# Attention stage of a fused attention and expert kernel: all 32 pairs written out in place of a loop on the engines

## The chip, the cores and the metric

The kernel runs on one core of a Trainium2 chip. Its engines each run their own instruction stream and meet at semaphores: TensorE (PE), VectorE (DVE), ScalarE (ACT), GpSimd (POOL) and SyncE (SP), the last for transfers alone. The metric is the device time of one execution in microseconds, the median of several runs; lower is better.

## The reference

One layer: cross attention with 16 heads of 8 dimensions over 64 batches of 64 tokens (D = 128), added to the input, and then a mixture of 8 experts with one expert per token, added again.

```python
x = x + xattn(_layernorm(x), ctx, ctx, mask, ...)     # H = 16, DK = 8
x = x + ffn(_layernorm(x), ...)

# xattn
scores = jnp.einsum('bhqd,bhkd->bhqk', q, k) * scale
scores = jnp.where(mask == 0, jnp.float32(-1000000000.0), scores)
attn = jax.nn.softmax(scores, axis=-1)
out = jnp.einsum('bhqk,bhkd->bhqd', attn, v)
return out.transpose(0, 2, 1, 3).reshape(query.shape[0], -1, D) @ Wo.T + bo

# ffn
router_probs = jax.nn.softmax(xt @ Wr + br, axis=-1)
gates = jnp.max(router_probs, axis=-1, keepdims=True)
idx = jnp.argmax(router_probs, axis=-1)
h = jax.nn.relu(jnp.einsum('te,td,edf->tf', onehot, xn, W1) + b1[idx])
y = (jnp.einsum('te,tf,efd->td', onehot, h, W2) + b2[idx]) * gates
```

## The kernel before

The 4096 tokens are worked on in 32 tiles of 128 tokens, each a pair of batches (NP = 32). The attention stage is a software pipeline over steps j: in step j every engine has a body `step(h, u)` with h = j // 2 and u = j % 2, and it works in it on several pairs at once, each in a different state. `pair(h, u, k)` gives the pair j + k, with its turn and its buffer (all tiles of the stage have two buffers).

In one step VectorE does, in this order: the layer norm's statistics of pair j + 3 (L489), the normalized tile xn of pair j + 2 (L495), the second layer norm of pair j - 4 (xt L501, row L503), the routing of pair j - 5 (L511 to L525), the row maxima of the scores of pair j (mx L535) and their subtraction (Pr L539), the division of the attention output of pair j - 2 (L546, L548), the residual and its statistics for pair j - 3 (L561 to L589) and the place in the table of pair j - 5 (L576 to L599). TensorE does the scores of pair j (L677, L681), eight transposes of the probabilities of pair j - 1 (L692), three transposes of xn, On and xt (L706 to L714), the output projection (L723), the router (L726), the ranks (L730, L731), probabilities times values of pair j - 2 (L738) and the projections for q, k and v (L752 to L757). ScalarE copies transposed tiles out of PSUM (L402, L409), takes the exponential (L419) and copies q, k and v (L424 to L434). GpSimd takes powers for the layer norms (rs L325, L336), adds the bias (L330), makes the blocks of k (Kb L341) and issues the indirect DMA that enters a token in a table (L349). SyncE loads x and the context (L226, L230, L234) and stores rows (L241).

The order of each engine is that of the code; nothing is scheduled by a planner. Each producer counts up a semaphore, and a consumer waits for a count that follows from the pair's number, for example `dve.wait_ge(s_s, p + 1)`.

`steps(eng, step, first, main, last, n)` (L49) lays these steps out. Steps before n * main[0] and from n * main[1] on are written out: h and u are numbers, and so are the counts waited for and the addresses. Between them stands a loop on the engine, `eng.Fori(main[0], main[1])`, whose body is n steps; there h is a register, and each count or address that follows from it is computed by the engine's sequencer. For the attention stage AM = (4, 13) and n = 2: nine turns of two steps, j = 8 to 25. Steps j = -3 to 7 and 26 to 36 are written out.

Behind it stands the stage of the experts with its own loops, over 39 slots of 128 tokens (`bstep`, `entries`, from about 296 us on).

Of the kernel before, what the change touches and what calls it, by code (L numbers as in the profile page):

```python
# [27 lines left out]
NP = T // P  # L28
# [14 lines left out]
def wait(eng, sem, value):  # L43

    if not (isinstance(value, int) and value <= 0):
        eng.wait_ge(sem, value)


def steps(eng, step, first, main, last, n):  # L49

    for j in range(first, n * main[0]):
        step(j // n, j % n)
    with eng.Fori(main[0], main[1]) as h:
        for u in range(n):
            step(h, u)
    for j in range(n * main[1], last):
        step(j // n, j % n)


def build(nc, x, ctxT, mask, wqT, bq, wkT, bk, wvT, bv, woT, bo, wr, br, ln_g, ln_b, w1, b1, w2, b2, out):  # L60
# [3 lines left out]
    with ExitStack() as ctx:  # L64
# [141 lines left out]

        block = ctx.enter_context(nc.Block())

        AM, A1 = (4, 13), NP + 5
        B0, BM, B1 = -2, (2, 9), SLOTS + 2  # L210

        def pair(h, u, k):
            p = at(h, u, k, 2)
            return None if isinstance(h, int) and not 0 <= p[0] < NP else p

        def slotn(h, u, k):
            s = at(h, u, k, R)
            return None if isinstance(h, int) and not 0 <= s[0] < SLOTS else s

        @block.sync  # L220
        def _(sp):
            def load(h, u):
                if (t := pair(h, u, 5)):
                    p, n, q = t
                    wait(sp, x_in[q], 16 * n)
                    sp.dma_start(X[:, bass.ds(p, 1), :], x[bass.ds(p * P, P), :].rearrange("t (o d) -> t o d", o=1)).then_inc(x_in[q], 16)  # L226
                if (t := pair(h, u, 4)):
                    p, n, q = t
                    wait(sp, s_pj, p - 1)
                    sp.dma_start(C[:, q, :], ctxT[:, bass.ds(p * P, P)]).then_inc(c_in[q], 16)  # L230
                if (t := pair(h, u, 2)):
                    p, n, q = t
                    wait(sp, s_pj, p + 1)
                    sp.dma_start(Cv[:, q, :], ctxT[:, bass.ds(p * P, P)]).then_inc(cv_in[q], 16)  # L234

            def step(h, u):
                load(h, u)
                if (t := pair(h, u, -4)):
                    p, n, q = t
                    sp.wait_ge(s_xt2, 2 * p + 2)  # L240
                    sp.dma_start(rows[bass.ds(p * P, P), :], row[:, q, :]).then_inc(r_out[q], 16)  # L241

            load(-3, 1)
            sp.dma_start(Wq[:], wqT).then_inc(s_w[0], 16)
            load(-2, 0)
            sp.dma_start(Wk[:], wkT).then_inc(s_w[0], 16)
            sp.dma_start(Wv[:], wvT).then_inc(s_w[0], 16)
            sp.dma_start(Wo[:], woT).then_inc(s_w[0], 16)
            load(-2, 1)
            for e in range(0, E, 2):  # L250
                sp.dma_start(W1[:, e:e + 2, :], w1[e:e + 2].rearrange("e d f -> d e f")).then_inc(s_w[3], 16)
                sp.dma_start(W2[:, e:e + 2, :, :], w2[e:e + 2].rearrange("e (c f) d -> f e c d", c=FC)).then_inc(s_w[3], 16)
            load(-1, 0)
            load(-1, 1)
            steps(sp, step, 0, AM, A1, 2)

            sp.wait_ge(s_slot, 1)
            for q in range(2):
                sp.wait_ge(r_out[q], 16 * (NP // 2))
                sp.wait_ge(e_out[q], 16 * (NP // 2))  # L260

            def entries(h, u):
                if (t := slotn(h, u, 0)):
                    s, n, q = t
                    wait(sp, e_in[q], 16 * n)
                    first = sp.value_load(slot[0:1, 1, bass.ds(s, 1)], min_val=0, max_val=ROWS - P)
                    sp.dma_start(ENT[:, bass.ds(s, 1), :], table[bass.ds(first, P), :].rearrange("t (o d) -> t o d", o=1)).then_inc(e_in[q], 16)

            steps(sp, entries, 0, (1, 9), SLOTS, R)
            for q in range(R):  # L270
                sp.wait_ge(o_out[q], 16 * len(range(q, SLOTS, R)))

        @block.gpsimd
        def _(pool):
# [75 lines left out]
                                         in_=ent[:, q, :], in_offset=None, bounds_check=last_entry,  # L350
                                         oob_is_err=False).then_inc(e_out[q], 16)

            steps(pool, step, -3, AM, A1, 2)

            def bstep(h, u):
                if (t := slotn(h, u, 2)):
# [18 lines left out]
        def _(act):  # L375
# [58 lines left out]
                            a.activation(VB[64 * h2:64 * h2 + 64, q, b, :, h2, 0:DK], src[:, :, h2, :],  # L434
                                         ACT.Copy).then_inc(s_v, 1)

            steps(act, step, -2, AM, A1, 2)

            act.wait_ge(s_slot, 1)
            act.wait_ge(s_w[3], 16 * (E + 2))  # L440
# [20 lines left out]
        def _(dve):  # L461
# [136 lines left out]
                    dve.wait_ge(s_pos, 6 * p + 3)  # L598
                    v.tensor_copy(posi[:, q, :], posf[:, q, :]).then_inc(s_pos, 1)  # L599

            steps(dve, step, -3, AM, A1, 2)


            k = [0]
# [56 lines left out]
        def _(pe):  # L661
# [96 lines left out]
                if last is not None:  # L758
                    last.then_inc(s_pj, 1)

            steps(pe, step, -2, AM, A1, 2)


            pe.wait_ge(s_rt, 7 * NP)
# [68 lines left out]
```

## Time and profile before

| | before |
|---|---|
| median of 3 runs | 470.75 us |
| lowest, highest | 468.31 us, 471.48 us |
| span of the profiled execution | 445.3 us |
| PE, DVE, ACT, POOL busy, share of the span | 75%, 68%, 46%, 47% |
| instructions profiled | 12096 |
| granted TensorE clock, mean | 0.822 |

The span goes from the first to the last instruction of the profiled execution; the time of a run is taken from outside and is longer. The granted clock is given as a share of full speed, 1.00 at 2.4 GHz and 0.50 at 1.2 GHz. Busy shares are means over two stages that have different limits, so a change in the attention stage is read from that stage alone, which takes from about 14 us to 296 us. VectorE's L535 occurs once for each pair, 32 times.

### The profile page before, as it was taken

What the parts mean: (1) busy time and instruction counts of PE and PEld (TensorE: products, weight loads), DVE (VectorE), ACT (ScalarE), POOL (GpSimd) and SP (SyncE); (2) the same over time, 40 slices, a digit from 0 to 9 for tenths busy, and PEclk for the clock granted to TensorE, in tenths of its full rate; (3) what the DMA queues carried; (4) which work ended last, traced back from release to release, by engine and by line L of the source; (5) the groups of instructions that cost most, each with busy time, mean ns of one, the idle gap of its engine ahead of it and who ended that gap; (6) DMA issues with size and microseconds to landing.
All of it is one profiled execution on the core that took longest, in us unless ns stands there. A gap on an engine that the chain in (4) does not pass through costs nothing.

```text
span 445.3 us, 12096 instructions
## 1 busy us (share of the span) xinstructions
PE 335.5 (75%) x2988; PEld 243.7 (55%) x2989; DVE 302.3 (68%) x1120; ACT 202.6 (46%) x588; POOL 207.4 (47%) x261
## 2 busy tenths in 40 slices
PE   0578879879889889898967886406888888888870
PEld 0356647658668668676745665303555655555550
DVE  3268999888988988988999895651454545444440
ACT  1158564644554554545565553001545454544540
POOL 5314354354354354354364523313576666666540
PEclk9999996685785775758699785555999999999996
DMA  5921121111111121111121100002222221122110
GB/s 141 381 70 51 33 52 40 35 55 30 30 59 30 30 59 30 30 53 36 35 45 35 32 25 24 26 0 48 55 53 69 59 60 51 59 65 59 50 31 0
DMA packets 35770, 23.64 MB, mean 53 GB/s; under 512 B 11599, under 2 KB 32724, under 8 KB 35744
## 3 DMA queue, kind: packets, MB, share of 16 engines
q1 hardware_dynamic: 29872, 14.99, 12.0%
q0 software_dynamic: 4272, 7.69, 5.9%
q10 hardware_dynamic: 1600, 0.65, 0.6%
q8 instruction: 12, 0.20, 0.3%
q14 instruction: 14, 0.11, 0.1%
HBM read 16.55 MB, written 7.22 MB: 53 GB/s over the span
## 4 chain that ended last, share of the span: by engine, by line
DVE 30%; issue 29%; PE 17%; POOL 7%; DMA 6%; ACT 3%; DVEq 3%; ACTq 1%; POOLq 1%; SPq 0%
PE ps L776 7%; DVE mx L535 6%; PE ps L784 6%; DMA G<-rows_dram,gi 4%; ACT xg L447 3%; DVE lsub L514 2%; DVE xt L501 2%; POOL rs L336 2%; DVE st L569 2%; DVE row L503 1%; DVE Pr L539 1%; PE ps L792 1%; DVE oh L522 1%; DVE rsum L546 1%; DVE st L489 1%
## 5 line engine op out<-in xcount | busy, mean ns | idle before, releaser
L336 POOL TENSOR_TENSOR rs<-ve,half 128x2 f32<-128x2 f32 x32 | 23.1, 723 | 107.3 <-DVE ve L589 103.9
L419 ACT ACTIVATE Pr<-Pr,rowany 128x1024 f32<-128x1024 f32 x32 | 36.7, 1148 | 65.1 <-DVE Pr L539 65.1
L644 DVE COPY hs<-ps 128x512 f32<-128x512 f32 x39 | 27.0, 692 | 52.3 <-PE ps L776 52.3
L368 POOL DMA_INDIRECT out<-ot,si x39 | 39.5, 1013 | 44.1 <-DVE gi L639 20.5
L776 PE MATMUL ps<-W,xg 128*128 x78 | 45.5, 666 | 17.1 <-ACT xg L447 17.1
L692 PE MATMUL ps<-ident,Pr 128*128 128x128 f32 x256 | 54.1, 350 | 2.0 <-ACT Pr L419 1.7
L784 PEld LDWEIGHTS ps<-W,hT 128*128 128x128 f32 x312 | 38.6, 192 | 25.4 <-issue 25.3
L455 ACT ACTIVATE hT<-ps,b1c 128x128 f32<-128x128 f32 x156 | 44.6, 369 | 16.2 <-PE ps L798 10.3
L402 ACT ACTIVATE PT<-ps 128x512 f32<-128x512 f32 x64 | 38.2, 598 | 26.2 <-PE ps L692 25.7
L692 PEld LDWEIGHTS ps<-ident,Pr 128*128 128x128 f32 x256 | 39.0, 180 | 19.5 <-issue 14.9
L361 POOL DMA_INDIRECT G<-rows_dram,gi x39 | 39.9, 1023 | 18.7 <-issue 11.0
L447 ACT ACTIVATE xg<-ps,cols 128x128 f32<-128x128 f32 x39 | 17.9, 458 | 63.6 <-PE ps L792 63.6
L738 PE MATMUL ps<-VB,PT 128*64 128x18 f32 x1024 | 45.3, 236 | 0.7 <-ACT GT L409 0.7
L784 PE MATMUL ps<-W,hT 128*128 x312 | 43.2, 282 | 0.8 <-ACT hT L455 0.7
L738 PEld LDWEIGHTS ps<-VB,PT 128*64 128x64 f32 x1024 | 42.0, 171 | 1.7 <-ACT GT L409 0.9
L535 DVE TENSOR_REDUCE mx<-ps 128x16 f32<-128x1024 f32 x32 | 39.1, 1221 | 3.0 <-PE ps L681 3.0
L539 DVE TENSOR_TENSOR Pr<-ps,mx 128x1024 f32<-128x1024 f32 x32 | 39.2, 1224 | 2.0
L349 POOL DMA_INDIRECT table_dram<-ent,posi x32 | 34.8, 1088 | 9.1 <-issue 3.7
L341 POOL TENSOR_TENSOR Kb<-KT,hmask 128x512 f32<-128x512 f32 x32 | 33.4, 1044 | 11.8 <-ACT KT L426 11.8
L409 ACT ACTIVATE GT<-ps 128x384 f32<-128x384 f32 (+2 forms) x38 | 16.7, 440 | 41.5 <-PE ps L714 32.0
L325 POOL TENSOR_TENSOR rs<-ve,half 128x1 f32<-128x1 f32 x32 | 18.0, 563 | 36.0 <-DVE ve L530 36.0
L706 PE MATMUL ps<-ident,xn 128*128 128x128 f32 x32 | 11.6, 363 | 24.5 <-DVE xn L495 24.5
(119 smaller groups left out, 679.0 us busy)
## 6 DMA issues: line engine op xcount, KB each, us to landing
W<-in_w SPq DMA_DIRECT2D x8, 512.0 KB, 8.7
rows_dram<-row SPq DMA_DIRECT2D x32, 128.0 KB
X<-in_x SPq DMA_DIRECT2D x32, 64.0 KB, 1.9
C<-in_ctxT SPq DMA_DIRECT2D x32, 64.0 KB
Cv<-in_ctxT SPq DMA_DIRECT2D x32, 64.0 KB, 2.0
ENT<-table_dram SPq DMA_DIRECT2D x39, 1.0 KB
G<-rows_dram,gi POOLq DMA_INDIRECT x39, 2.8
out<-ot,si POOLq DMA_INDIRECT x39, 2.3
```

The lines of the kernel that those rows point to most:

```text
L349: g.indirect_dma_start(out=table, out_offset=bass.IndirectOffsetOnAxis(ap=posi[:, q, :], axis=0), in_=ent[:, q, :], in_offset=None, bounds ...
L361: g.indirect_dma_start(out=G[:, q, :], out_offset=None, in_=rows, in_offset=bass.IndirectOffsetOnAxis(ap=gi[:, q, :], axis=0), bounds_chec ...
L368: g.indirect_dma_start(out=out, out_offset=bass.IndirectOffsetOnAxis(ap=si[:, q, :], axis=0), in_=ot[:, q, :], in_offset=None, bounds_chec ...
L402: a.activation(PT[:, q, 512 * m:512 * m + 512], ps[:, 4 + m, :], ACT.Copy).then_inc(s_pt, 1)
L419: a.activation(Pr[:, q, :], Pr[:, q, :], ACT.Exp, scale=rowany[:, 0:1]).then_inc(s_p, 1)
L455: a.activation(hT[:, q % 2, P * c:P * c + P], ps[:, 2 + q % 2, P * c:P * c + P], ACT.Relu, bias=b1c[:, bass.ds(ex * FC + c, 1)]).then_inc( ...
L535: v.tensor_reduce(out=mx[:, q, :].rearrange("p (g i) -> p g i", i=4), in_=sc, axis=AX.X, op=ALU.max).then_inc(s_sm, 1)
L539: v.tensor_tensor(out=Pr[:, q, :].rearrange("p (g i k) -> p g i k", g=4, k=S), in0=sc, in1=mx[:, q, :].rearrange("p (g i) -> p g i", i=4)[ ...
L692: last = nc.tensor.transpose(ps[:, 4 + m, 128 * j:128 * j + 128], Pr[:, q, 128 * (4 * m + j):128 * (4 * m + j) + 128], ident[:])
L738: last = mm(psPV[64 * b:64 * b + 64, 18 * j:18 * j + 18], PT[:, q, 128 * j + 64 * b:128 * j + 64 * b + 64], VB[:, q, b, j, :, :].rearrange ...
L776: mm(ps[:, q % 2, :], xg[:, q, :], W1[:, bass.ds(ex, 1), :].rearrange("p e f -> p (e f)"), start=True, stop=True).then_inc(b_up, 1)
L784: last = mm(ps[:, 6 + q % 2, 0:D], hT[:, q % 2, P * c:P * c + P], W2[:, bass.ds(ex, 1), c, :].rearrange("p e d -> p (e d)"), start=(c == 0 ...
```

## The change

The loop of the attention stage is taken away on all five engines. Each engine now has all its steps written out with h and u as numbers. The bodies are the same, and the loops of the expert stage stay. The same two lines replace the call of `steps` on SP, POOL, ACT, DVE and PE; the first step is 0, -3, -2, -3 and -2.

```diff
-        AM, A1 = (4, 13), NP + 5
+        A1 = NP + 5
...
-            steps(sp, step, 0, AM, A1, 2)
+            for j in range(0, A1):
+                step(j // 2, j % 2)
...
-            steps(dve, step, -3, AM, A1, 2)
+            for j in range(-3, A1):
+                step(j // 2, j % 2)
```

What this moves is seen in each engine's instructions. First VectorE, at the entry of the loop (step j = 8), kernel before. The rows read line, instruction, output and inputs, and in brackets the semaphores that are waited for; ISA and REGISTER_ALU rows are register work of the sequencer.

```order
L599 CAST posi<-posf 128x1 [waits places]
L53 UNCONDITIONAL_BRANCH
L53 ISA
L489 ISA [waits x_in1]
L489 BN_STATS st<-X 128x6
L490 ISA
L46 REGISTER_ALU [waits ln1_rstd,ln1_stats]
L495 ISA [waits step_transposed]
L495 TENSOR_SCALAR xn<-X,mv,rs 128x128
L499 ISA
L46 REGISTER_ALU [waits ln2_rstd]
L501 TENSOR_SCALAR xt<-row,mv,rs 128x128 [waits step_transposed]
```

The same place in the changed kernel, whose line numbers are three higher here:

```order
L602 CAST posi<-posf 128x1 [waits places]
L492 BN_STATS st<-X 128x6 [waits x_in1]
L498 TENSOR_SCALAR xn<-X,mv,rs 128x128 [waits step_transposed,ln1_rstd,ln1_stats]
L504 TENSOR_SCALAR xt<-row,mv,rs 128x128 [waits step_transposed,ln2_rstd]
L506 TENSOR_SCALAR row<-row,mv,rs 128x128
```

The arithmetic instructions and the semaphores they wait for are the same ones; the branch and the register rows between them are gone.

TensorE at its entry of the loop, kernel before:

```order
L757 MATMUL ps<-Wv,Cv 128x128 [waits cv_in1]
L53 UNCONDITIONAL_BRANCH
L53 ISA
L46 REGISTER_ALU [waits k_blocks,q_copied]
L677 MATMUL ps<-pen,eye 128x256 [waits softmax_shift]
L677 MATMUL ps<-pen,eye 128x256 x3
L681 MATMUL ps<-Kb,QT 64x256 x8
L689 ISA
L46 ISA [waits probs]
L692 MATMUL ps<-ident,Pr 128x128 [waits pT_copied]
L692 MATMUL ps<-ident,Pr 128x128 x3
```

And in the changed kernel, line numbers four higher:

```order
L761 MATMUL ps<-Wv,Cv 128x128 [waits cv_in1]
L681 MATMUL ps<-pen,eye 128x256 [waits softmax_shift,k_blocks,q_copied]
L681 MATMUL ps<-pen,eye 128x256 x3
L685 MATMUL ps<-Kb,QT 64x256 x8
L696 MATMUL ps<-ident,Pr 128x128 [waits pT_copied,probs]
L696 MATMUL ps<-ident,Pr 128x128 x3
```

Here too the matrix products follow in the same order with the same waits; the waits that stood on register rows (k_blocks with q_copied, and probs) now stand on the instructions themselves.

## Rows read from the trace of the kernel before

**Rows 1.** The page, its first line.

```profile
span 445.3 us, 12096 instructions
```

**Rows 2.** Timeline of VectorE, starts of L535: start us, duration us, engine, line.

```profile
67.39 1.21 DVE L535 TENSOR_REDUCE mx<-ps 128x16 f32<-128x1024 f32 x1
...
226.67 1.21 DVE L535 TENSOR_REDUCE mx<-ps 128x16 f32<-128x1024 f32 x1
...
234.08 1.22 DVE L535 TENSOR_REDUCE mx<-ps 128x16 f32<-128x1024 f32 x1
```

**Rows 3.** Stretches: length, busy PE, PEld, DVE, ACT, POOL, clock, DMA, GB/s.

```profile
59.98:67.39 7.41, 5.55 (x78) 4.02 (x76) 7.02 (x31) 4.27 (x14) 3.83 (x5) 1.00 0.19 42
151.60:159.95 8.35, 8.35 (x74) 6.63 (x74) 7.17 (x29) 3.73 (x10) 3.82 (x5) 0.50 0.14 39
159.95:168.43 8.48, 6.43 (x81) 4.97 (x80) 7.56 (x29) 4.88 (x15) 3.82 (x5) 0.90 0.14 39
226.67:234.08 7.41, 5.54 (x78) 4.02 (x76) 7.02 (x30) 4.25 (x14) 3.82 (x5) 1.00 0.19 33
241.49:249.24 7.75, 5.67 (x78) 4.06 (x76) 7.18 (x28) 4.39 (x14) 4.28 (x6) 1.00 0.10 27
249.24:257.01 7.77, 7.70 (x71) 5.88 (x72) 6.91 (x25) 3.53 (x10) 3.31 (x4) 0.56 0.16 44
```

**Rows 4.** Timeline of VectorE, in the loop and behind it; idle before in brackets.

```profile
164.60 0.15 DVE L599 CAST posi<-posf 128x1 int32<-128x1 f32 x1
164.85 0.29 DVE L489 BATCH_NORM_STATS2 st<-X 128x6 f32 x1
165.34 0.93 DVE L495 TENSOR_SCALAR xn<-X,mv,rs 128x128 f32 x1 [0.20 <-DVE st L489]
...
173.56 0.29 DVE L489 BATCH_NORM_STATS2 st<-X 128x6 f32 x1 [0.54 <-issue]
...
230.81 0.14 DVE L599 CAST posi<-posf 128x1 int32<-128x1 f32 x1
230.87 0.28 DVE L489 BATCH_NORM_STATS2 st<-X 128x6 f32<-128x128 f32 x1
...
236.47 0.24 DVE L546 RECIPROCAL rsum<-ps 128x16 f32<-128x16 f32 x1
...
246.34 1.05 DVE L501 TENSOR_SCALAR xt<-row,mv,rs 128x128 f32<-128x128 f32 x1 [0.29 <-POOL rs L336]
```

**Rows 5.** Timeline of TensorE, in the loop at low clock and behind it.

```profile
185.16 1.90 PE L738 MATMUL ps<-VB,PT 128*64 128x18 f32 x32
...
193.98 1.90 PE L738 MATMUL ps<-VB,PT 128*64 128x18 f32 x32
...
229.28 0.59 PE L677 MATMUL ps<-pen,eye 64*128 64x256 bf16 x4 [0.60 <-DVE Pr L539]
...
231.68 0.30 PE L706 MATMUL ps<-ident,xn 128*128 128x128 f32 x1 [0.59 <-DVE xn L495]
...
232.62 0.33 PE L714 MATMUL ps<-ident,xt 128*128 128x128 f32 x1 [0.54 <-DVE xt L501]
...
234.12 1.11 PE L738 MATMUL ps<-VB,PT 128*64 128x18 f32 x32
```

**Rows 6.** Stretches before, in and behind the loop, columns as in group 3.

```profile
24.30:68.50 44.20, 36.95 (x472) 26.91 (x472) 38.06 (x115) 28.53 (x77) 19.03 (x27) 1.00 0.16 44
...
75.40:218.70 143.30, 126.12 (x1276) 99.08 (x1276) 125.16 (x477) 73.56 (x204) 64.92 (x85) 0.69 0.14 39
218.70:249.50 30.80, 22.98 (x313) 16.77 (x313) 28.96 (x112) 17.82 (x51) 15.82 (x21) 1.00 0.15 36
```

**Rows 7.** DMA queues: packets, MB, share; 24:68, then 84:218, then landings.

```profile
q8 instruction: 4, 0.07, 0.5%
q14 instruction: 3, 0.02, 0.2%
...
q14 instruction: 1, 0.01, 0.0%
...
X<-in_x SPq DMA_DIRECT2D x32, 64.0 KB, 1.9
```

More of the change, by code:

```diff
@@ L351, in step @@
                                          oob_is_err=False).then_inc(e_out[q], 16)
-            steps(pool, step, -3, AM, A1, 2)
+            for j in range(-3, A1):
+                step(j // 2, j % 2)
             def bstep(h, u):
@@ L435, in step @@
                                          ACT.Copy).then_inc(s_v, 1)
-            steps(act, step, -2, AM, A1, 2)
+            for j in range(-2, A1):
+                step(j // 2, j % 2)
             act.wait_ge(s_slot, 1)
@@ L599, in step @@
                     v.tensor_copy(posi[:, q, :], posf[:, q, :]).then_inc(s_pos, 1)
-            steps(dve, step, -3, AM, A1, 2)
+            for j in range(-3, A1):
+                step(j // 2, j % 2)
             k = [0]
@@ L759, in step @@
                     last.then_inc(s_pj, 1)
-            steps(pe, step, -2, AM, A1, 2)
+            for j in range(-2, A1):
+                step(j // 2, j % 2)
             pe.wait_ge(s_rt, 7 * NP)
```

## The prediction

> **What bounds the kernel now.** I read the page first for where the time lies. The profiled execution spans 445.3 us [rows 1]; the median of the runs is 470.75 us (468.31 to 471.48), so 25.45 us lie outside the span, and I take them as untouched. Then I took the vector engine's timeline and followed one instruction, the maximum over the scores (L535). It runs once per step, so its starts are the clock of the attention stage. Where the same steps are written out, behind the loop, one takes 234.08 - 226.67 = 7.41 us [rows 2]. Next to it I put the table by stretches, with the starts of L535 as bounds, so that each row is one step [rows 3]. The reader is to see two paces in it: 7.41 us with VectorE busy for 7.02 of them where steps are written out, and 8.35 and 8.48 us with 7.17 and 7.56 busy for the two steps of a turn of the loop (16.83 us, 8.41 a step). Written-out steps leave VectorE 0.4 us of idle time, the loop's 1.0 us on average.
>
> Third, what fills that time. In a written-out step the statistics of the next tile (L489) start 0.06 us after the cast before them, at 230.81 and 230.87 [rows 4]. In the loop they start 0.25 us after it in one step (164.60, 164.85) and the next instruction another 0.49 us later with 0.20 us idle; at the turn of the loop L489 stands idle 0.54 us with "issue" named, which is no other engine but the sequencer's own register work. So VectorE sets the pace in both forms, and the loop's form is paced by what VectorE's sequencer has to work out ahead of its instructions.
>
> TensorE is not the bound at its high clock. In a written-out step it is idle 0.60, 0.59 and 0.54 us, each time for VectorE, 1.73 us in all [rows 5]. At its low clock it is different: from one L738 to the next it takes 193.98 - 185.16 = 8.82 us, with the row before each following straight on. That is more than 7.41. This is the one thing that could take the gain back.
>
> **The change part by part.** It removes the loop from five engines and writes 18 steps (j = 8 to 25) out. As the order shows, every arithmetic instruction keeps its place and its waits; the branch and the register rows go. Nothing is moved past a queue: each DMA stays behind the same wait.
>
> - VectorE, the pace: from the last L535 ahead of the loop's influence to the first behind it there are 226.67 - 67.39 = 159.28 us and 19 intervals (pair 7 to pair 26) [rows 2]. 19 x 7.41 = 140.79 us. The gain is 159.28 - 140.79 = 18.49 us. This needs no price of a single register operation; it takes a row of the same step in the other form.
> - PE, ACT, POOL and SP lose register rows too. Nothing of that is on the path: PE waits for VectorE in the rows above, and POOL's and ACT's long waits end on VectorE as well. Their cover is VectorE's 7.02 us of work in 7.41; if it went, POOL would be next, since xt (L501) already waits 0.29 us for POOL's power (L336) in the stage's last steps [rows 4].
> - The low clock. The trace shows 44.2 us at 1.00 ahead of the loop and 30.8 us at 1.00 behind it, and 0.69 on average in the 143.3 us of the loop [rows 6]; 0.50 is the lower of the two levels (1.2 GHz). What does a low stretch cost at the new pace? PE falls behind by 1 - 7.41/8.82 = 0.16 us per us. The one inside written-out steps lies in the interval 249.24 to 257.01 at mean 0.56, so (1 - 0.56)/0.5 = 0.88 of 7.77, 6.8 us low, and puts PE 1.09 us behind. VectorE reads L738's result at 236.47 [rows 4], and L738 was done at 234.12 + 1.11 = 235.23 [rows 5], a slack of 1.24 us, so that one is free, and its interval of 7.77 us beside 7.75 us for the same kind of step at 1.00 [rows 3] bears this out. From below the price is nothing. From above: the loop has (1 - 0.69)/0.5 = 62% low time, 10.4 us in each turn of 16.83. A low stretch of 10.4 us puts PE 1.66 us behind, and L738 itself takes 1.90 instead of 1.11, which leaves 0.45 of slack: 1.2 us lost. 140.8 us hold 9.5 such pairs of steps, 11.4 us. I take 1.0 us, near the lower end, because the nearest rows are those of the written-out steps: about 82 us of them with the low stretch of one step at each end, so three or four in 141 us, at 0.3 us each.
>
> Code has to be fetched. In the 44 us of written-out steps there are 4 and 3 transfers of instructions, in 134 us of the loop one [rows 7]. 7/44 x 140.8 = 22 of them are to be expected, some 0.09 MB in each 44 us. I cost them at nothing since the step from 59.98 to 67.39 in that stretch keeps 7.41 us [rows 3]; the cover is that they land before their code is due, and its price if it is gone stands under the rivals.
>
> Sum: -18.49 + 1.0 = -17.5 us. 470.75 - 17.5 = 453.2 us.
>
> **The rivals.**
> - A, the forecast: 7.41 us a step with few low stretches, gain 16.5 to 18.5, 452 to 454 us. For it: the same steps at the same pace on both sides of the loop. 0.70.
> - B, TensorE's clock stays as low as in the loop, and at a pace of 7.41 PE can no longer hide it: 11.4 us of the gain come back, 470.75 - 18.5 + 11.4 = 463.7 us; with half of that, 458. For it: 44.2 us at 1.00 is the longest stretch of the stage without a fall [rows 6], and the stage is now 141 us of the same steps, with PE's work in each no larger. Against: 75 us of written-out steps show one fall at their end each, 62% low was seen only in the loop. 0.13.
> - C, the steps settle at the 7.75 us of the stage's last ones, where VectorE waits for POOL [rows 3, 4]: 19 x 7.75 = 147.3, gain 12.0, 458.7 us. A low clock could shift POOL's multiply into VectorE's short instructions. Against: the full steps have fallen into 7.41 each time they were written out. 0.08.
> - D, the change does less than it says: the register work was hidden and only the turn goes. Nine turns at the 0.54 us of idle time that L489 has there are 4.9 us, 465.9 us. Against: both steps of a turn are slow (8.35 and 8.48), not only the one with the branch. 0.04. The Trainium skill ("Advanced Engine Details and Errata", Control Flow Timing) gives about 108 ns for a compare-and-branch; by that figure alone nine turns would be worth 1 us, an estimate, and the time 469.8. The row's 0.54 us is five times that, so here the branch is not what the turn costs.
> - E, slower: the written-out code is fetched too late and an engine stands. A transfer of 64 KB lands in 1.9 us [rows 7]. 22 fetches at 1.9 us, each whole on the path, are 42 us: 494 us. It decides from 18.49/22 = 0.84 us a fetch on. Against it is the pace of the written-out steps. 0.02. The Trainium skill ("Advanced Engine Details and Errata", ISA Cache) speaks for this rival: the instruction store of most engines is two lines of 256 instructions, so a loop can run out of it and written-out code has to be brought in. The trace shows that it is brought in, and no engine that stands for it.
> - The remaining 0.03: a gain above 21 us, which would need a step below 7.3 us.
>
> **How the numbers follow.** The measurement of this kernel tells about 1% (4.7 us) from no change. A, B, C and the last case are faster by more, and D by 4.9 us stands on the line: faster 0.93, same 0.05, slower 0.02. The range goes down to the lowest run less the gain, 468.31 - 18.5 = 449.8, so 449.5, and up past C and half of B to 461. That leaves out B's upper half, D, E and part of A's spread.
>
> **What would show it.** Step right: L535 starts every 7.41 us from 52 to about 220 us, L489 starts within 0.1 us of the cast before it, and the stage behind begins some 17 to 18 us earlier. Low clock right: the intervals with a mean near 0.5 are at most 0.3 us longer; wrong if "rsum L546" or "mx L535" shows idle time that ends on PE. Code fetch right: some 20 more instruction transfers and no idle "issue" on VectorE above 0.1 us. The prediction is wrong if the steps keep 8.4 us without the register rows, or if POOL's L336 stands ahead of L501 in each step.

## The result

The changed kernel takes 455.67 us, the median of four runs (448.75 to 460.1); the kernel before took 469.53 us (466.35 to 471.48; three of its four runs are those of the forecast's base). The ratio is 0.963 with a 95% interval of 0.9527 to 0.9733; it compares fast executions alone and leaves out the two longest runs of the changed kernel (457.47 and 460.1 us) as slow ones, where the plain medians stand at 0.970. The forecast was 453.2 us, a ratio of 0.963 to its base of 470.75. The median came out 2.5 us above it and inside the range, but outside the 452 to 454 us of its own case A. The reasons behind it hold in part only, as the traces show.

The page of the changed kernel: its span, busy times, granted clock in 40 slices, and the queues that bring instructions. Its trace is of the longest of the four runs, 460.1 us.

```profile
span 458.3 us, 11009 instructions
...
PE 336.7 (73%) x2988; PEld 242.5 (53%) x2989; DVE 298.4 (65%) x1120; ACT 202.1 (44%) x588; POOL 206.9 (45%) x261
...
PEclk9999996785858959667668755569899999999995
...
q8 instruction: 22, 0.36, 0.5%
...
q14 instruction: 22, 0.18, 0.2%
```

The arithmetic instructions are those of before; 1087 instructions of other kinds are gone (12096 to 11009). The span is longer than that of before (458.3 against 445.3 in [rows 1]), although the kernel is faster. That is the first thing to explain. With 460.1 us for the time of this execution, 1.8 us lie outside the span, not 25.

Here are two views that say where the spans differ. L644 of the kernel before (L648 after) is VectorE's copy in each of the 39 slots of the expert stage; min, median and max of its duration in ns, then its first and last start. First the kernel before, from the same trace as the rows ahead of the prediction.

```profile
L644 DVE COPY hs<-ps x39: 690/692/693, 307.0 to 429.9; 128x512 f32<-128x512 f32 x39
```

The changed kernel:

```profile
L648 DVE COPY hs<-ps x39: 690/692/693, 301.6 to 443.0; 128x512 f32<-128x512 f32 x39
```

The expert stage begins 5.4 us earlier after the change, but then takes 141.4 us from first to last start against 122.9. Its code is the same in both. So either the change slows the stage behind it, or one of the two traces is not typical. The experiments have to say which.

The attention stage of the changed kernel, by stretches with the starts of L538 (the old L535) as bounds: length, busy PE, PEld, DVE, ACT, POOL, clock, DMA share, GB/s. The first row is the step ahead of what was the loop, the second the 19 intervals from pair 7 to pair 26, the last three single steps among them.

```profile
60.04:67.46 7.42, 5.55 (x78) 4.03 (x77) 7.04 (x31) 4.27 (x14) 3.83 (x5) 1.00 0.17 35
67.46:217.74 150.28, 133.54 (x1424) 101.20 (x1423) 134.66 (x535) 81.10 (x228) 72.43 (x95) 0.73 0.18 44
...
100.75:108.16 7.41, 7.41 (x71) 5.83 (x70) 7.03 (x30) 2.74 (x10) 3.81 (x5) 0.50 0.15 39
108.16:117.10 8.94, 8.91 (x76) 6.93 (x75) 7.12 (x30) 4.26 (x13) 3.81 (x5) 0.50 0.17 44
117.10:125.21 8.11, 7.16 (x97) 5.42 (x95) 7.20 (x30) 5.96 (x17) 3.95 (x6) 0.98 0.16 44
```

These 19 intervals are called the stretch below. It takes 150.3 us. It took 159.3 before [rows 2], and 140.8 were expected. A step of 7.41 us is there, even at the low clock (100.75 to 108.16, all of it at 0.50, PE busy without a break). The next one, still at 0.50, takes 8.94. So the pace of the written-out form is as forecast, and something adds 9.5 us to it in single steps.

What adds it stands in VectorE's waits from 68 to 218 us of the changed kernel: total, times, longest, in us. L549, L564 and L742 are the lines L546, L561 and L738 of the kernel before; "issue" is idle time for which no other engine is named.

```profile
DVE rsum L549 <- PE ps L742: 4.7, 7, 1.5
DVE row L564 <- DMA rows_dram<-row: 2.7, 1, 2.7
DVE ve L591 <- issue: 0.3, 1, 0.3
DVE mx L538 <- issue: 0.2, 1, 0.2
```

These are 7.9 of the 9.5 us. VectorE's own busy time, 134.66 us in 19 intervals or 7.09 each against 7.04 in the step ahead, is another 0.9.

And in VectorE's timeline, the places where they fall (idle time in brackets):

```profile
73.16 0.29 DVE L564 TENSOR_TENSOR row<-ps,xb 128x128 f32<-128x128 f32 x1 [2.75 <-DMA rows_dram<-row]
...
74.55 0.14 DVE L602 CAST posi<-posf 128x1 int32<-128x1 f32 x1
74.60 0.28 DVE L492 BATCH_NORM_STATS2 st<-X 128x6 f32<-128x128 f32 x1
...
112.07 0.26 DVE L549 RECIPROCAL rsum<-ps 128x16 f32<-128x16 f32 x1 [1.44 <-PE ps L742]
```

The register work is gone: L492 follows the cast after 0.05 us, where the loop took 0.25 us or stood idle for 0.54 [rows 4]. Two other waits are there. At 112.07 the low clock is in the path: VectorE waits 1.44 us for probabilities times values. At 73.16 VectorE waits 2.75 us to write into the buffer row, because the store that reads it has not landed. TensorE's timeline shows the first of the two from its side:

```profile
110.12 1.90 PE L742 MATMUL ps<-VB,PT 128*64 128x18 f32 x32
111.96 0.80 PE L756 MATMUL ps<-GT,Wq 128*128 128x128 f32 x2
```

L742 starts at 110.12 and takes 1.90 us, as it did at the low clock in the loop [rows 5]; at 112.02 it is done and VectorE goes on 0.05 us later.

The second wait is not in a step that the change touches. It belongs to the step j = 7, the last one ahead of the loop, which is written out in the kernel before as well. This is the same place in the trace of the kernel before, with the issue of the store, the write into row (L561) and the first instruction of the loop:

```profile
62.89 0.43 SPq L241 DMA_DIRECT2D rows_dram<-row  x1
...
70.27 0.28 DVE L561 TENSOR_TENSOR row<-ps,xb 128x128 f32<-128x128 f32 x1
...
71.99 0.29 DVE L489 BATCH_NORM_STATS2 st<-X 128x6 f32 x1 [0.21 <-issue]
```

From the issue of the store of pair 2 to the moment at which VectorE needs its buffer again, 7.4 us pass before the change and 7.5 after it (issue at 62.95, L564 ready at 70.41). The slack is the same, so the shorter steps have not caused this wait.

### The profile page after: what moved, and what is told of

Same layout as the page of the kernel before. It is cut to its first block, busy times and chain, and to the rows that moved or that the text cites. A ratio compares the mean times of both kernels' runs of the same rounds, so it can differ in the third digit from the quotient of the medians.

```text
span 458.3 us, 11009 instructions
## 1 busy us (share of the span) xinstructions
PE 336.7 (73%) x2988; PEld 242.5 (53%) x2989; DVE 298.4 (65%) x1120; ACT 202.1 (44%) x588; POOL 206.9 (45%) x261
## 4 chain that ended last, share of the span: by engine, by line
issue 38%; PE 24%; POOL 14%; DVE 8%; DMA 7%; ACT 3%; ACTq 2%; POOLq 1%; DVEq 0%; another core or an unknown queue 0%; SPq 0%
PE ps L781 7%; PE ps L789 7%; POOL table_dram L350 5%; PE ps L797 4%; POOL rs L337 3%; DMA G<-rows_dram,gi 3%; ACT xg L450 2%; POOL xb L331 2%; POOL Kb L342 2%; DMA rows_dram<-row 2%; POOL rs L326 1%; PE ps L742 1%; DMA Wr<-in_wr 1%; DVE Pr L542 1%; DVE mx L538 1%
## 5 line engine op out<-in xcount | busy, mean ns | idle before, releaser
L337 POOL TENSOR_TENSOR rs<-ve,half 128x2 f32<-128x2 f32 x32 | 24.7, 771 | 112.5 <-DVE ve L592 109.6
L648 DVE COPY hs<-ps 128x512 f32<-128x512 f32 x39 | 27.0, 692 | 48.2 <-PE ps L781 44.3
L789 PEld LDWEIGHTS ps<-W,hT 128*128 128x128 f32 x312 | 39.6, 195 | 27.3 <-issue 27.3
L458 ACT ACTIVATE hT<-ps,b1c 128x128 f32<-128x128 f32 x156 | 44.5, 368 | 19.2 <-PE ps L803 10.2
L789 PE MATMUL ps<-W,hT 128*128 x312 | 44.3, 286 | 1.9 <-ACT hT L458 1.3
L742 PE MATMUL ps<-VB,PT 128*64 128x18 f32 x1024 | 44.3, 233 | 0.3 <-ACT GT L411 0.3
L742 PEld LDWEIGHTS ps<-VB,PT 128*64 128x64 f32 x1024 | 41.0, 167 | 1.3 <-ACT GT L411 0.5
L538 DVE TENSOR_REDUCE mx<-ps 128x16 f32<-128x1024 f32 x32 | 38.9, 1216 | 3.7 <-PE ps L685 3.5
L350 POOL DMA_INDIRECT table_dram<-ent,posi x32 | 34.8, 1087 | 9.2 <-issue 5.0
L781 PEld LDWEIGHTS ps<-W,xg 128*128 128x128 f32 x78 | 12.0, 194 | 38.1 <-issue 38.0
L504 DVE TENSOR_SCALAR xt<-row,mv,rs 128x128 f32<-128x128 f32 x32 | 27.5, 858 | 5.9 <-POOL rs L337 4.3
```

Source lines behind the costliest of these rows:

```text
L337: g.tensor_tensor(out=rs2[:, q, :], in0=ve2[:, q, :], in1=half[:], op=ALU.pow).then_inc(s_r2, 1)
L350: g.indirect_dma_start(out=table, out_offset=bass.IndirectOffsetOnAxis(ap=posi[:, q, :], axis=0), in_=ent[:, q, :], in_offset=None, bounds ...
L458: a.activation(hT[:, q % 2, P * c:P * c + P], ps[:, 2 + q % 2, P * c:P * c + P], ACT.Relu, bias=b1c[:, bass.ds(ex * FC + c, 1)]).then_inc( ...
L538: v.tensor_reduce(out=mx[:, q, :].rearrange("p (g i) -> p g i", i=4), in_=sc, axis=AX.X, op=ALU.max).then_inc(s_sm, 1)
L742: last = mm(psPV[64 * b:64 * b + 64, 18 * j:18 * j + 18], PT[:, q, 128 * j + 64 * b:128 * j + 64 * b + 64], VB[:, q, b, j, :, :].rearrange ...
L781: mm(ps[:, q % 2, :], xg[:, q, :], W1[:, bass.ds(ex, 1), :].rearrange("p e f -> p (e f)"), start=True, stop=True).then_inc(b_up, 1)
```

## The experiments

There are three questions: is it VectorE's register work that set the pace; what do the low clock and the store cost at the new pace; and is the expert stage slower for the change? Most of these kernels have one trace, of one execution. How much one kernel varies is seen in the two traces of before (159.3 and 159.2 us for the stretch) and the three of the changed kernel (150.3, 145.5 and 142.8).

**Both kernels again.** First the changed kernel unchanged.

> The changed kernel once more, unchanged, to see which of its longer steps come back. In its first trace 19 steps took 150.3 us where 140.8 were forecast; 5.2 us of the excess stand in waits of VectorE for TensorE (L549) in low clock stretches and 2.8 us in one wait for the store of row (L564). If the low clock is the cause, the waits at L549 come back with about the same sum, 3 to 6 us, since the work of TensorE is the same. If late landings are chance, the waits at L564 lie elsewhere or are absent. The expert stage took 171 us there against 149 in the trace of before with the same code: if that is chance, it comes out shorter than 165 here; if the written-out code shifts it for good, it stays near 171.

Measured: 454.36 us (453.47 to 455.13), ratio 0.9807 (0.9717 to 0.9896) to the 464.65 us that the kernel before took beside it. The stretch takes 145.5 us, of which 58.3 us at the low clock. The waits at L549 sum to 1.3 us and not to the 3 to 6 expected. The wait for row stands at the same place as in the first trace (1.90 us at 72.31), not elsewhere.

Then the kernel before.

> The kernel before once more, unchanged. The attention stage should repeat to within 1 us (31st L535 at about 264 us, turns of 16.8 us), since its pace in the loop is VectorE's. If the expert stage has several paces of its own whatever the attention stage does, its length should differ from the 149 us of the first trace; if it is fixed by the code, it is 149 us again.

Measured: 465.8 us against 464.65, ratio 1.0043 (0.9993 to 1.0092). The stretch takes 159.2 us, as in the first trace. The two kernels again, in VectorE's copy of the expert stage; first before:

```profile
L644 DVE COPY hs<-ps x39: 690/691/693, 307.3 to 444.0; 128x512 f32<-128x512 f32 x39
```

and the changed one:

```profile
L648 DVE COPY hs<-ps x39: 690/692/693, 295.8 to 436.4; 128x512 f32<-128x512 f32 x39
```

The expert stage takes 136.7 us in one and 140.6 in the other. So the changed kernel keeps its length, which the expectation took as a sign of the change, but the kernel before now has nearly the same one. In twelve of the thirteen traces of this study it takes 136.7 to 145.0 us, in loop and written-out forms alike (the loop form with idle products, below, took 142.7); the trace ahead of the prediction, with 122.9, is the exception. That trace was the odd one: an execution of 445.3 + 1.8 = 447.1 us, below the lowest timed run. The start of the expert stage is free of this: 307.0 and 307.3 us before, 301.6, 295.8 and (below) 292.2 after, so the attention stage gives 5 to 15 us. The medians are 10 to 16 us apart. In the stretch alone the three traces of the changed kernel gain 9.0, 13.7 and 16.4 us; by the start of the expert stage 3.6, 2.2 and 1.6 us of that are lost again. Of these, 3.1, 1.1 and 0.7 us go between pair 26 and the last pair, in steps that are written out in both kernels, and the rest ahead of the stretch or behind the last pair. From 218 to 262 us VectorE waits 0.5, 3.8 and 2.2 us for L742, where the two traces of before have 0 and 0.4, and in the first trace 1.61 us more for row (at 230.44).

**VectorE alone written out.** This is the kernel before with VectorE's call replaced; SP, POOL, ACT and PE keep the loop:

```diff
-            steps(dve, step, -3, AM, A1, 2)
+            for j in range(-3, A1):
+                step(j // 2, j % 2)
```

> Only VectorE's steps are written out, the other four engines keep the loop. Theory of the prediction: VectorE's sequencer sets the pace, so this has nearly the whole gain: steps of 7.4 to 7.6 us and an attention stage as short as in the changed kernel or shorter (L535 of the last pair at 250 to 258 us), with few instruction transfers added (about 5). Rival, that the other engines' register work is as slow: steps stay above 8 us. Rival, that fetching TensorE's code makes landings late: here no wait for the store of row.

Measured: 450.81 us, ratio 0.9725 (0.9606 to 0.9843). Beside it the changed kernel took 454.36 (ratio 0.9807), and the two intervals overlap, so the medians do not tell whether writing out the other four engines is worth anything. The stretch takes 144.7 us, most steps 7.49 (columns as above):

```profile
67.90:212.64 144.74, 119.52 (x1430) 88.17 (x1429) 135.54 (x535) 81.78 (x231) 72.43 (x95) 0.88 0.16 44
```

**All but VectorE written out**, the other half of the same edit.

> All engines but VectorE written out. Theory of the prediction: no gain in the attention stage, turns of 16.8 us, ratio 0.995 to 1.005 apart from the expert stage. Rival, that each engine's loop costs a part: steps between 7.4 and 8.4 us.

Measured: 463.07 us, ratio 0.9979 (0.993 to 1.0027). The stretch takes 158.2 us. In VectorE's timeline of this kernel the loop's idle times are all there:

```profile
157.38 0.15 DVE L602 CAST posi<-posf 128x1 int32<-128x1 f32 x1
158.07 0.29 DVE L492 BATCH_NORM_STATS2 st<-X 128x6 f32 x1 [0.54 <-issue]
158.61 0.44 DVE L498 TENSOR_SCALAR xn<-X,mv,rs 128x128 f32 x1 [0.25 <-DVE st L492]
```

So the gain is VectorE's: its sequencer's register work paced the loop. Writing out the other four engines alone brings 1 us in the stretch (158.2 against 159.2), and nothing that the medians can tell.

**Four buffers for row.** The changed kernel with two more buffers and their semaphores, so that L564 waits for the store of four pairs earlier and not of two:

```diff
-        row = sb("row", [P, 2, 2 * D])
+        row = sb("row", [P, 4, 2 * D])
...
-                    wait(dve, r_out[q], 16 * n)
-                    v.tensor_tensor(out=row[:, q, 0:D], in0=psO, in1=xb[:, q, :], op=ALU.add).then_inc(s_x1, 1)
+                    wait(dve, r_out[p % 4], 16 * (p // 4))
+                    v.tensor_tensor(out=row[:, p % 4, 0:D], in0=psO, in1=xb[:, q, :], op=ALU.add).then_inc(s_x1, 1)
```

> The changed kernel with four buffers for the tile row in place of two, so that the residual (L564) waits for a store issued four pairs earlier. Theory, late landings of the store of row cost the 1.9 to 4.4 us seen in single steps: no wait for rows_dram<-row is left, and the 19 steps between pair 7 and pair 26 lose 2 to 3 us, to about 143 to 147 us. Waits at L549 for TensorE stay at 3 to 6 us. Rival, that the late landings only come through at another wait (x for the statistics, the context for TensorE): the stage keeps its length and a wait of the same size stands at L492 or in TensorE.

Measured: 450.91 us, ratio 0.9631 (0.9572 to 0.9691). The trace has no wait at this line; the stretch takes 144.9 us with 58.0 us at the low clock, and the waits for probabilities times values are 2.5 us, a little under the 3 to 6 expected. This does not show that the buffers removed the wait: the third trace of the changed kernel and the one with idle products, both below, have two buffers and no wait either.

**Idle products on TensorE.** The changed kernel with 20 more products a step, whose results are overwritten (here called idle products, since they are put where PE stands idle), so that PE does the same work for the kernel and some beside it:

```diff
+                        for _ in range(10 * (1 - m)):
+                            mm(ps[:, 4, 0:128], ones[:], before[:], start=True, stop=True, skip_group_check=True)
...
+                    for _ in range(10):
+                        mm(ps[:, 6, 256:384], ones[:], before[:], start=True, stop=True, skip_group_check=True)
```

> The changed kernel with 20 idle products (bf16, 128x128 by 128x128, results overwritten) per step on TensorE, ten ahead of the first transposes of probabilities and ten ahead of the transpose of xt, where it stands idle 0.59 and 0.54 us a step at the high clock. Theory, low clock stretches cost the waits at L549: the low time between pair 7 and pair 26 falls from 58 to 80 us to under 20, waits at L549 under 1 us, steps 7.41, the stage 3 to 6 us shorter. Rival, the extra products are themselves too much: TensorE takes about 1 us longer a step, and steps grow to 7.6 us or more in all stretches.

Measured: 451.17 us, ratio 0.9657 (0.96 to 0.9714). The stretch from pair 7 to pair 26 in this kernel:

```profile
69.40:211.00 141.60, 126.87 (x1808) 99.77 (x1806) 133.64 (x534) 80.83 (x230) 72.43 (x95) 0.98 0.20 47
```

The clock is 0.98 and the 19 intervals take 141.6 us, 0.8 above the 140.8 of the forecast at full clock. PE is busy for less time than in the first trace of the changed kernel (126.87 us against 133.54), though it does more. In the median nothing of this shows: the ratios of the changed kernel are 0.963, 0.9807 and 0.9652. The same stretch of the changed kernel's second trace, without the idle products:

```profile
67.40:213.00 145.60, 125.47 (x1426) 94.52 (x1427) 134.18 (x535) 81.62 (x230) 72.54 (x95) 0.80 0.17 45
```

**Both together**, four buffers and idle products.

> Both: four buffers for row and the idle products. If both causes are what they seem and independent, the 19 steps take 141 to 143 us, close to the 140.8 of 19 times 7.41, and the time is 6 to 9 us below the changed kernel's in this job.

Measured: 449.91 us, ratio 0.9598 (0.9508 to 0.9689); the stretch takes 141.6 us again. It is the lowest median, but its interval overlaps those of the two kernels before it, so which is best is open. The changed kernel was not run beside it, so the expected 6 to 9 us below that kernel cannot be read off.

**The loop kept, with idle products.** This asks whether the low clock cost the kernel before anything.

> The kernel before, loop kept, with the same idle products. Theory: in the loop the low clock costs nothing, since a turn of 16.8 us hides TensorE at 8.82 us a step nearly whole, so the low time falls and the steps stay at 8.41 us, ratio 0.995 to 1.005. Rival, that the clock costs in the loop too: a stage 2 us or more shorter.

Measured: 468.09 us, ratio 1.0014 (0.9978 to 1.0049). The stretch:

```profile
69.50:228.80 159.30, 123.80 (x1807) 96.91 (x1808) 139.82 (x534) 80.29 (x229) 72.63 (x95) 1.00 0.15 40
```

At 1.00 throughout, where [rows 6] has 0.69, the stretch takes the same 159.3 us with the loop. In the loop VectorE's register work hid the low clock fully; the written-out form no longer hides it.

**VectorE alone written out, with idle products.**

> VectorE alone written out, the other engines in the loop, and 20 idle products a step on TensorE (they add work whose results are overwritten). Two causes were named for the part of the gain that is missing: the low clock, and the late landing of the store of row. Theory 'low clock is the rest': the stretch from pair 7 to pair 26 takes 141 to 143 us (VectorE written out alone took 144.7 with 34 us low), low time under 10 us, no wait at L564 for the store; ratio about 0.965. Rival 'the loop on the other engines also costs': the stretch stays at 144 to 146 us although the clock is high, because PE's, ACT's or POOL's register work now stands in VectorE's waits; then writing out all five engines is worth the difference to 141.6.

Measured: 454.79 us, ratio 0.9714 (0.962 to 0.9807). The stretch takes 143.1 us, none of it at the low clock, nearly all in steps of 7.49 and 7.50. Both theories hold a part: without the low clock 1.6 of the 144.7 us go, and 1.5 us (143.1 against 141.6) remain as what the loop on the other four engines costs, 0.08 us a step.

**The changed kernel a third time.**

> The changed kernel unchanged. Both its traces so far show a wait at L564 for the store of row (idle 2.75 and 1.61 us in one, 1.90 in the other) early in the stage, and low stretches. Theory 'late landing belongs to the written-out form': again a wait at L564 of 1 to 3 us at about 72 us and a stretch from pair 7 to pair 26 of 145 to 150 us. Rival 'it is chance of an execution': no such wait, and the stretch then takes 144 us or less. Ratio to the kernel before 0.965 to 0.98 by both.

Measured: 453.6 us, ratio 0.9652 (0.9561 to 0.9743). The stretch takes 142.8 us, 41.0 of them at the low clock. VectorE's waits from 68 to 218 us, as shown of the first trace above:

```profile
DVE rsum L549 <- PE ps L742: 0.7, 2, 0.4
DVE ve L591 <- issue: 0.3, 1, 0.3
DVE mx L538 <- issue: 0.2, 1, 0.2
```

There is no wait at L564, and of the 4.7 us for PE 0.7 are left. So the rival's statement holds for the wait: it comes with one execution and not with another.

**VectorE alone written out, a second time.**

> VectorE alone written out, a second look. Theory 'late landing belongs to the written-out form of all engines, whose instructions are fetched by the same queues': no wait at L564 over 0.3 us. Rival 'chance of an execution': a wait of 1 us or more shows up in this one. Stretch from pair 7 to pair 26 144 to 146 us.

Measured, a single run: 458.86 us. The stretch takes 148.7 us with 58.0 at the low clock, above what either theory expected. The wait that was absent from the first trace of this kernel is there:

```profile
72.85 0.29 DVE L561 TENSOR_TENSOR row<-ps,xb 128x128 f32<-128x128 f32 x1 [1.53 <-DMA rows_dram<-row]
...
89.11 0.26 DVE L546 RECIPROCAL rsum<-ps 128x16 f32<-128x16 f32 x1 [1.48 <-PE ps L739]
```

So the wait for the store does not belong to the code of the other engines. Three traces have it at 72 to 73 us (the first again at 230): two of the three of the changed kernel, and one of the two of VectorE alone written out. It comes and goes with the execution, and each time it stands in a step that is written out in both kernels.

The landings that the traces record say more. A store lands in 16 parts. In the first trace of the changed kernel fourteen parts of the store of pair 2 land from 67.51 to 68.92 us, the last two at 72.95 and 73.04, which is 10.1 us after the issue. This one store is late in all thirteen traces, before and after: its last recorded part comes 4.7 to 10.1 us after the issue, where the median store of the attention stage has landed after 1.7 to 2.2 us. In the trace of before it took 5.0 of the 7.4 us of slack; 10.1, 9.2 and 8.3 us are the three traces with the wait. With four buffers it took 4.9, which two buffers would have covered as well.

## Why the prediction was right, and where it was not

The traces of the stretch side by side, worked out from the starts of L535 (L538 or L539 where the line has moved) and the granted clock:

| kernel | stretch, us | low clock in it, us | wait for row in it, us |
|---|---|---|---|
| before, two traces | 159.3, 159.2 | 95.6, 94.4 | none |
| before, idle products | 159.3 | 0.0 | none |
| all but VectorE written out | 158.2 | 98.3 | none |
| VectorE alone, two traces | 144.7, 148.7 | 34.1, 58.0 | none, 1.5 |
| VectorE alone, idle products | 143.1 | 0.0 | none |
| changed, three traces | 150.3, 145.5, 142.8 | 79.8, 58.3, 41.0 | 2.75, 1.9, none |
| changed, four buffers | 144.9 | 58.0 | none |
| changed, idle products | 141.6 | 6.8 | none |
| changed, both | 141.6 | 10.2 | none |

- **What bounds the kernel, and 7.41 us a step: right.** VectorE alone written out has most of the shortening, all the others without it about 1 us. At a clock of 0.98 the 19 intervals take 141.6 us against 140.8 forecast.
- **The other engines' loop costs nothing: right to 1.5 us** of 18.5 once VectorE is fast (143.1 against 141.6, one trace each), and to 1 us while it is not.
- **The low clock, 1.0 us: mis-sized, and this is the step that failed.** The term took its price from the short stretches at the ends of the written-out steps and expected three or four of one step each. In the first trace of the changed kernel the low stretches last 13.7 to 17.1 us, and the trace of before already held one as long (columns as in [rows 3]):

```profile
184.60:201.70 17.10, 17.10 (x150) 13.56 (x149) 14.95 (x58) 8.32 (x24) 7.63 (x10) 0.50 0.13 38
```

By the prediction's own rate (0.16 us per us, 0.45 us of slack with the longer L738) a stretch of 17.1 us costs 2.3 us; the one from 100.4 to 117.5 us cost 1.5 in the interval of 8.94 us and 0.4 in that of 8.11 (which takes 7.73 in the trace at 0.98), together 1.9. So the rate was about right, the length was not. From the level of 141.6 us, with the wait for row taken off, what is left for the clock is 5.9, 2.0 and 1.2 us in the three traces and 3.2 with four buffers: on average 3.1 where 1.0 was taken. Of these, 4.7, 1.3, 0.7 and 2.5 us stand as waits for L742; the rest is a difference. The prediction had named this wait as the sign that the term is wrong. It is a part of rival B, whose half was 5.7 us; B's upper price of 11.4 us was itself too high, since it put the 10.4 us of low clock that two looped steps hold in 16.8 us into every two written-out steps, which last 14.8.
- **The wait for row: not in the prediction, and not of the change either.** It adds 2.75, 1.9 and 0 us to the stretch in the three traces, in a step that both kernels have written out with the same slack. None of the four traces with VectorE in the loop has the wait and three of the nine with VectorE written out have it, which may be chance; why the store lands late is open. What the prediction left out is the slack: from [rows 7] I had the 1.9 us in which X lands and took no landing of a store, and in that same trace the store of pair 2 took 5.0 of its 7.4 us. In the steps that do change the least slack falls from 6.0 us to 4.8 in the first trace, and no wait for row stands there in any trace.
- **Fetching the code at no cost: nearly right.** The page shows 22 and 22 instruction transfers where before has 12 and 14. The longest idle "issue" of VectorE in the stretch is 0.27 us, above the 0.1 that the prediction allowed. It stands at L591, and 0.23 us stand at L538, in the same two steps of all nine traces with VectorE written out; these steps take 7.73 and 7.76 us at a clock of 0.98, which is 0.7 of the 0.8 us above 140.8. An instruction transfer begins 0.6 to 1.9 us behind each, but that the idle time is the price of fetching is not shown, and the kernel before has 0.39 us of the same kind at L588. Rival E falls. The Trainium skill ("Advanced Engine Details and Errata", ISA Cache) has two lines of 256 instructions for most engines; the trace agrees in that written-out code is brought in again and again, and shows that it comes early enough but for what these two places may cost.
- **Rival C (7.75 us by POOL): not seen.** There is no wait for POOL in VectorE's list from 68 to 218 us. **Rival D (only the turn, 4.9 us): excluded**, since the stretch became 9.0 to 16.4 us shorter and both steps of a turn with it.
- **Case A, the forecast's own: reached by pace, not by size.** It had a gain of 16.5 to 18.5 us, and the stage behind was to begin some 17 to 18 us earlier. The stretch gained 9.0, 13.7 and 16.4 us, and the expert stage began 5.4, 11.5 and 14.8 us earlier.
- **25.45 us outside the span: wrong.** The time of each run whose span is known is about 1.8 us above it. The trace of before was that of an execution with a short expert stage. The error did not reach the sum, since the gain came from the attention stage alone, and its stretch takes 159.3 and 159.2 us in the two traces of before. Had a term been read from the expert stage, it would have carried a fault of 14 to 22 us.

So the gain in the stretch was 9.0, 13.7 and 16.4 us, 13.1 on average, where 17.5 were forecast, and the medians gave 13.9, 10.3 and 16.0. There is luck in how close the time came. The base of 470.75 us was the highest median of before that was measured (469.53, 464.65, 467.05, 469.56 later); from 464.65 the same sum gives 447.1, where 454.36 was measured. The changed kernel's ratio was 0.963 once and 0.9807 and 0.9652 later, and of the shortfall in the first two traces 2.75 and 1.9 us are the wait for row, which was not forecast.

## What to carry to other kernels

Read the same step in its looped and its written-out form in one trace; the difference is the price of the loop, with no need to price a register operation, and only the engine that paces the stage has to be written out for nearly the whole gain. When the pace falls, ask of every wait that the old pace hid, here a lower clock of another engine, what slack is left, and size it by the longest case in the trace, not the nearest. Before a new wait is put down to the change, look whether the step in which it stands was changed at all. Before a span is set against a median, see whether the profiled execution is a typical one.

## What the runs showed that was not expected

- The granted clock of the same code differs from execution to execution: it is low for 79.8, 58.3 and 41.0 us of the stretch in three traces of the changed kernel. Some 20 small idle products a step raise it from 0.73 to 0.86 up to 0.98 (1.00 in the loop), with PE busy for less time in all than in the first trace (126.87 us against 133.54) and about as long as in the second (125.47). The first trace also holds a step in which PE was busy for 7.41 of 7.41 us at 0.50, and the next one stayed at 0.50 (108.16 to 117.10, 8.91 us busy).
- One store of 128 KB, that of pair 2, lands late in all thirteen traces, 4.7 to 10.1 us after its issue where the median is 1.7 to 2.2, and in the first trace of the changed kernel two of its 16 parts land 4 us behind the others. What holds it is open; it is late with the loops and with the written-out code of every engine.
- The expert stage took 122.9 us in one trace and 136.7 to 145.0 in twelve others, of the same code. Why was not tried.
